# A two-layer gated cross-attention and feed-forward block on one core: a key projection, an addition, a scaling and the terms of a value tile change places

## The reference

```python
x = x + tanh(g_xattn[0]) * _L0_xattn_ref(layernorm(x), ctx, ...)  # fake_quant(x1) @ fake_quant(ctx), 8 bits
x = x + tanh(g_ffn[0])   * _L0_ffn_ref(layernorm(x), W_int, scale_i32, bias)   # per-token 8 bit, dequantized W, + bias
x = x + tanh(g_xattn[1]) * _L1_xattn_ref(layernorm(x), ctx, ctx, Wq, Wk, Wv, Wo)  # 32 heads of 32, 8 KV heads
x = x + tanh(g_ffn[1])   * _L1_ffn_ref(layernorm(x), weight_packed, scales)    # 4 bit weights

def fake_quant(x, scale, zp):
    q = jnp.clip(jnp.round(x / scale + zp), 0.0, 255.0)
    return (q - zp) * scale
```

## Time and profile before

| what | value |
|---|---|
| median of 3 runs | 850.35 us (848.24 to 850.78) |
| the profiled execution, its own time | 850.95 us |
| span of its records, first to last instruction | 849.1 us |
| TensorE (matmul) | 822.5 us, 97% of the span |
| VectorE | 590.0 us, 69% |
| GpSimd | 536.4 us, 63% |
| ScalarE | 448.9 us, 53% |
| mean granted clock of TensorE | 0.996 of full speed |

### The profile page before, as it was taken

The page is one execution under the profiler, slowest core; times in us unless marked ns, Lnnn a source line. Parts: engine busy times, 40 slices in busy tenths (PEclk is TensorE's granted clock), DMA queues, the critical chain, the costliest instruction groups (busy, mean ns, idle before and its releaser), DMA issues.

```text
span 849.1 us, 14036 instructions
## 1 busy us (share of the span) xinstructions
PE 822.5 (97%) x4498; PEld 332.2 (39%) x4498; DVE 590.0 (69%) x850; ACT 448.9 (53%) x742; POOL 536.4 (63%) x235
## 2 busy tenths in 40 slices
PE   8999989899999999999999999999999889999998
PEld 7766634344444432222222222222222213444443
DVE  5897768988378678888888888888888400555522
ACT  4445466565422257767777777777777771111200
POOL 5556158956243437988888988888988885222300
PEclk9999999999999999999999999999999999999999
DMA  7999953428995116445456444546544434122331
GB/s 251 230 288 293 278 123 108 105 57 151 251 231 152 64 59 135 109 103 107 105 113 134 109 108 100 121 96 133 127 96 94 100 63 87 25 50 49 62 137 74
DMA packets 120823, 107.81 MB, mean 127 GB/s; under 512 B 85325, under 2 KB 105805, under 8 KB 116685
## 3 DMA queue, kind: packets, MB, share of 16 engines
q1 hardware_dynamic: 115120, 71.59, 32.7%
q0 software_dynamic: 4608, 33.56, 19.5%
q10 hardware_dynamic: 1052, 2.10, 0.9%
HBM read 41.55 MB, written 12.58 MB: 64 GB/s over the span
## 4 chain that ended last, share of the span: by engine, by line
PE 65%; DMA 10%; POOL 8%; DVE 5%; issue 4%; DVEq 3%; ACT 3%; SPq 1%; ACTq 0%; POOLq 0%
PE sbank L1673 9%; PE sbank L1684 9%; PE mpair L1613 9%; POOL wraw L604 7%; DMA tail<-wraw 5%; PE sbank L1483 3%; PE sbank L1485 3%; PE sbank L1484 3%; PE sbank L1751 3%; PE sbank L1768 3%; PE sbank L1753 3%; PE sbank L1766 3%; PE sbank L1755 3%; DVEq L958 3%; DMA regD<-wraw 3%
## 5 line engine op out<-in xcount | busy, mean ns | idle before, releaser
L1345 DVE TENSOR_REDUCE mx<-mpair 128x1 f32<-128x1024 f32 x256 | 302.3, 1217 | 60.8 <-PE mpair L1613 59.8
L900 ACT ACTIVATE regC<-sbank 128x512 f32<-128x512 f32 x512 | 277.9, 595 | 105.8 <-PE sbank L1673 102.6
L1673 PE MATMUL sbank<-regD 98*128 98x512 f16 x512 | 178.2, 384 | 6.6 <-ACT regC L900 5.6
L604 POOL TENSOR_TENSOR wraw<-regC 128x2048 f32<-128x2048 f32 x32 | 148.5, 4641 | 31.4 <-DMA tail<-wraw 24.7
L1613 PE MATMUL mpair<-regD 96*128 96x512 f16 x512 | 155.9, 380 | 1.0 <-DVE mx L1345 0.4
L1684 PE MATMUL sbank<-regC,regD 128*32 128x512 f32 x1024 | 136.4, 605 | 1.0 <-ACT regC L900 1.0
L1673 PEld LDWEIGHTS sbank<-regD 98*128 98x128 f16 x512 | 48.5, 97 | 184.8 <-ACT regC L900 147.3
L604 POOL TENSOR_TENSOR regD<-regC 128x2048 f32<-128x2048 f32 x16 | 76.5, 4781 | 13.6 <-ACT regC L900 13.5
L604 POOL TENSOR_TENSOR tail<-regC 128x2048 f32<-128x2048 f32 x16 | 77.0, 4814 | 0.0
L1613 PEld LDWEIGHTS mpair<-regD 96*128 96x128 f16 x512 | 47.6, 98 | 54.4 <-DVE mx L1345 13.9
L497 POOL TENSOR_SCALAR xT_lo<-xT_lo,sc 128x1024 f32<-128x1024 f32 x16 | 31.1, 1944 | 36.4 <-DVE X L1010 28.2
(11 more groups left out here) (186 smaller groups left out, 1282.1 us busy)
## 6 DMA issues: line engine op xcount, KB each, us to landing
regD<-wraw POOLq DMA_DIRECT2D x16, 1024.0 KB, 7.0
tail<-wraw POOLq DMA_DIRECT2D x16, 1024.0 KB, 7.0
xT_lo<-in_ctx SPq DMA_DIRECT2D x16, 512.0 KB, 5.1
wraw<-in_L_ffn_W_int SPq DMA_DIRECT2D x8, 512.0 KB, 4.3
X<-in_x SPq DMA_DIRECT2D x4, 1024.0 KB, 7.0
wraw<-in_L_xattn_Wq SPq DMA_DIRECT2D x8, 512.0 KB, 3.7
wraw<-in_L_xattn_Wo SPq DMA_DIRECT2D x8, 512.0 KB, 4.3
regD<-q_hi_scratch SPq DMA_DIRECT2D x32, 128.0 KB, 2.4
```

The lines of the kernel that those rows point to most:

```text
L604: nc.gpsimd.tensor_tensor(p_sum[pr if pr < 3 else 1][:, :, :], probs[:, (2 * pr) % 4, :, :], probs[:, (2 * pr) % 4 + 1, :, :], ALU.add).th ...
L900: nc.scalar.activation(probs[:, kt % 4, h, :], bank[4 + h % 2], ACT.Exp, scale=SCALE).then_inc(s["exp_ok"], 1)
L1345: v.tensor_reduce(mx[m][:, bass.ds(n, 1)] if par is not None else mx[m][:, n:n + 1], slot[:, :, :], AX.XY, ALU.max).then_inc(s["mx_red"], 1)
L1673: pe.matmul(bank[4 + h % 2], kst[par][0:98, kt * P:(kt + 1) * P], qst[par][0:98, h * 512:(h + 1) * 512], start=True, stop=True).then_inc(s ...
```

## The change

Six edits, none of which changes what is computed.

1. TensorE: `k_proj(3, 1)` and the weight transposition 7 come ahead of the four column sums instead of behind them. ScalarE and VectorE follow: `k_out(3, 1)` and `k_low(3, 1)` come right behind those of key tile 0, the copies of the sums are split in two pairs and put between the steps of the last two tiles' norm, the weight tile 7's parts move back (`wd_low`) and its scaling forward (`wd_scale`).
2. GpSimd: the context passes of tiles 11 and 15 also wait for the affine values of the pair of x tiles that is in work; `add_c2(1)`, and with it all adds after tile 0, waits for the last of the eight roundings.
3. The scaling of the bias moves from VectorE (after a2's statistics) to ScalarE (after the rounding of tile 1). On ScalarE `wq_high(0)` moves ahead of the first deviation, `wq_high(1)` behind it, and none is left after the first rounding.
4. VectorE, chunks 1 and 2: `ctx_low(u + 3)` moves ahead of the second `stats` and `ln1_affine`.
5. `newton`: the reciprocal is also written to a PSUM column (`rr_p`), and the small products that read two SBUF operands read this one instead.
6. TensorE: the first value tile does, for each half of the depth, the products with the high half of the weights first, and waits for the low half only then.

```diff
@@ GpSimd: ctx_affine, add_c2
+                if u > 2 * TB and u % TB == TB - 1:
+                    pool.wait_ge(s["ln1_aff"], u // TB - 1)
                 nc.gpsimd.tensor_scalar(cx[:, u % TB, :], cx[:, u % TB, :], IS2, Z2, ALU.mult, ALU.add)
...
                 pool.wait_ge(s["ln1_u"], t + 1)
+                if t == 1:
+                    pool.wait_ge(s["ln1_q"], T)
                 nc.gpsimd.tensor_tensor(X[:, t, :], X[:, t, :], c2[:, t // TB, :], ALU.add).then_inc(s["x_c2"], 1)
@@ ScalarE: last chunk
             k_out(c, 0, False)
             ln1_out(T - 3)
-            for n in range(2 * B):
-                c2_out(n)
-            wd_high(T - 1)
+            k_out(c, 1, False)
             ln1_affine(T - 2)
+            c2_out(0)
+            c2_out(1)
             ln1_out(T - 2)
             ln1_affine(T - 1)
-            k_out(c, 1, False)
+            wd_high(T - 1)
             ln1_out(T - 1)
+            c2_out(2)
+            c2_out(3)
@@ ScalarE: stages A and B
+            def bias_scale():
+                act.wait_ge(s["bias_in"], 16)
+                nc.scalar.activation(biasB, biasB, ACT.Copy, scale=TF0).then_inc(s["bias_ok"], 1)
+
+            wq_high(0)
             ln2_deviation(0)
-            wq_high(0)
+            wq_high(1)
             for t in range(T):
                 ln2_round(t)
+                if t == 1:
+                    bias_scale()
...
-                if t < 5:
+                if 1 <= t < 5:
                     wq_high(t + 1)
@@ VectorE: chunk
                 wd_low(2 * c + 1)
+                ctx_low(u + 3)
                 stats(2 * c - 1, 2 * c - 1).then_inc(s["ln1_stat"], 1)
                 d()
                 ln1_affine(c - 1)
-                ctx_low(u + 3)
                 ctx_round(u + 2)
@@ VectorE: last chunk
             wd_low(T - 2)
+            wd_scale(T - 1)
             ln1_stats(c - 1)
             ln1_affine(c - 1)
-            wd_scale(T - 1)
             ln1_round(T - 4)
             ln1_stats(c)
             ln1_round(T - 3)
             ln1_affine(c)
             k_low(c, 0)
-            wd_low(T - 1)
+            k_low(c, 1)
             ln1_round(T - 2)
             ln1_round(T - 1)
-            k_low(c, 1)
-            def bias_scale():
-                dve.wait_ge(s["bias_in"], 16)
-                v.tensor_scalar(biasB, biasB, TF0, None, ALU.mult).then_inc(s["bias_ok"], 1)
-                d()
+            wd_low(T - 1)
@@ VectorE: newton, ln3_affine
                 v.reciprocal(rr[:, c], sd[:, c])
-                d()
-                v.tensor_tensor(ra_p[:, c], rr[:, c], rr[:, c], ALU.mult)
+                v.reciprocal(rr_p[:, c], sd[:, c])
+                d()
+                v.tensor_tensor(ra_p[:, c], rr_p[:, c], rr[:, c], ALU.mult)
...
-                v.scalar_tensor_tensor(out=mr_p[:, c], in0=mv[:, c, 0], scalar=0.5, in1=rr[:, c], op0=ALU.mult,
+                v.scalar_tensor_tensor(out=mr_p[:, c], in0=mv[:, c, 0], scalar=0.5, in1=rr_p[:, c], op0=ALU.mult,
@@ TensorE: first value tile, called instead of v_proj(0, 0)
+            def first_v_proj():
+                pe.wait_ge(s["ct_lo"], 2)
+                for half in range(2):
+                    if half == 1:
+                        ctx_turn(1, 2)
+                    ks = range(4 * half, 4 * half + 4)
+                    pe.wait_ge(s["wkv_hi"], half + 1)
+                    for k in ks:
+                        pe.matmul(bank[0][:, 0:KV], ctxT_hi[:, k, 0:P], wv_hi[:, k, :], start=(k == 0), stop=False)
+                        pe.matmul(bank[0][:, 0:KV], ctxT_lo[:, k, 0:P], wv_hi[:, k, :], start=False, stop=False)
+                    pe.wait_ge(s["wkv_lo"], half + 1)
+                    for k in ks:
+                        m = pe.matmul(bank[0][:, 0:KV], ctxT_hi[:, k, 0:P], wv_lo[:, k, :], start=False,
+                                      stop=(k == KD - 1))
+                m.then_inc(s["kv_mm"], 1)
@@ TensorE: chunks 1 to 3
                 k_proj(c, 0)
-                if last:
-                    for n in range(2 * B):
-                        c2_sum(n)
-                wd_turn(2 * c + 1)
+                if not last:
+                    wd_turn(2 * c + 1)
                 k_proj(c, 1)
+            wd_turn(KD - 1)
+            for n in range(2 * B):
+                c2_sum(n)
```

More of the change, by code:

```diff
@@ L169, in build @@
                   + [("b", t) for t in range(3, T)])
-        ra_p, am_p, step_p, mr_p, rh_p = (bank[7][:, T * i:T * i + T] for i in range(5))
+        ra_p, am_p, step_p, mr_p, rh_p, rr_p = (bank[7][:, T * i:T * i + T] for i in range(6))
         acc_sb = y[:, 0:512]
@@ L1287, in _ @@
                 a_stats(t)
-                if t == 2:
-                    bias_scale()
             ln2_scales(0)
@@ L1495, in v_proj @@
                     pe.wait_ge(ctl[n % 2], 16 * (n // 2 + 1))
-                if u == 0:
-                    pe.wait_ge(s["wkv_lo"], 1)
                 if c > 0:
@@ L1501, in v_proj @@
                     pe.wait_ge(s["ct_lo"], 2 * j)
-                def between(i):
-                    if u == 0 and i == 2:
-                        ctx_turn(1, 2)
-                        pe.wait_ge(s["wkv_lo"], 2)
                 t0 = (c % 2) * 512
@@ L1509, in v_proj @@
                       lambda k: ctxT_lo[:, k, bass.ds(t0 + j * P, P)], lambda k: wv_hi[:, k, :],
-                      lambda k: wv_lo[:, k, :], between).then_inc(s["kv_mm"], 1)
+                      lambda k: wv_lo[:, k, :]).then_inc(s["kv_mm"], 1)
+            def first_v_proj():
[13 more added lines that the diff above has]
+                m.then_inc(s["kv_mm"], 1)
             def k_proj(c, m):
@@ L1544, in _ @@
             idle_products(12)
-            v_proj(0, 0)
+            first_v_proj()
             ctx_turn(2, 4)
```

## The result

| | before | after |
|---|---|---|
| median, us (executions) | 850.94 (8) | 843.44 (8) |
| lowest to highest, us | 847.9 to 853.8 | 841.13 to 847.49 |
| profiled execution: its own time, us | 850.95 | 841.13 |
| ratio after to before | | 0.9912, 95% interval 0.9893 to 0.9931 |

The change wins 7.5 us in the medians; forecast were 7.1 and 843.3 us. The profiled execution of after is the fastest of its eight, so the two profiles stand 9.8 us apart, more than the change is worth. To read them, I cut each at two starts of TensorE: that of the first product of stage A, and that of the first product of the query projection (its line is L1483 before and L1490 after).

What follows compares the result with a forecast made beforehand. TensorE, 97% busy, could win only idle and half-clock time, chiefly a 3.9 us key-tile wait, then VectorE's in-order chain. -3.9 - 1.7 - 2.1 + 1.0 - 0.4 = -7.1 us gave 843.3 us; eight times in ten 841.1 to 847.0.

Steps and rivals of the forecast that it cites:

- My own sign of being wrong: Wait over 2 us at first B or fourth A product behind it, front losing over 2, or query projection not moving.
- The wait of the second product, -3.9: Stage A: with the last key projection ahead of the sums, TensorE's 3.9 us wait for the key tile goes.
- The held adds: GpSimd, stage A: adds held behind the eighth rounding cause no wait; that rounding takes 0.69 us rather than 2.44.
- The clock, -1.7: Behind the second A product's wait: clock stays up, its 16 matmuls fall to 3.5 us; bounds 0 and -1.9.
- VectorE's chain, -2.1: Stage A to B: of 3.6 us of later TensorE waits, 1.5 stay lost to clip collisions; bounds -3.6 and +4.
- The small multiply: VectorE's chain to stage B: 2.08 us becomes 0.16 with one PSUM operand, plus a 0.17 reciprocal; 1.8 us saved.
- the bias scale: Moved to ScalarE: VectorE then waits about 1.3 us for ScalarE, so only some 0.2 of 1.5 us are won.
- Context subtraction, +1.0: Front, chunks 1 and 2: moved forward it delays the affine chain and weight scale; 1.0 us lost, bounds 0 and +2.0.
- First value tile, -0.4: Front: high-half products fill TensorE's 1.0 us wait for the low half; part is eaten later; bounds 0 and -2.7.
- B: Stages A and B: clip collisions on VectorE's chain take back half, gain 4.3 us, 846.0 us; chance 0.17.
- C: Nothing measurable, under 2.55 us, about 849.5: query projection waits for low transfers behind the last clip, or order fails; chance 0.09.
- D: Slower: GpSimd becomes the bound with 50 us of work from 116.7 on; 853.4 us at 13 us late; chance 0.03.

Runs made afterwards that it cites:

- the second pair: Second profiles: the changed kernel run again unchanged (median 844.61 us) beside the kernel before run once more (852.02 us, one execution).
- e1: Kernel before with only the new order of the last key projection, on all engines: 848.9 us against 852.1, ratio 0.9956.
- e2: Changed kernel with the order of the last key projection put back, other five edits kept: 846.07 us, ratio to before 0.9927.
- e7: Changed kernel without the hold of GpSimd's adds behind the last rounding: 847.7 us against 851.06 for the kernel before, ratio 0.9948.
- e12: Changed kernel run again unchanged, on a third chip: 844.61 us, ratio to before 0.9916.
- e4: Changed kernel with the first value tile in its old order: 844.53 us, ratio to before 0.9915.
- e9: Changed kernel with the context subtraction back behind the affine step and the weight scale ahead of VectorE's rounding: 843.78 us, ratio to before 0.9913.
- e8: Changed kernel with the small multiplies as before, both operands in SBUF and no second reciprocal: 850.11 us, ratio to before 0.9982.

## Why the prediction was right, step by step

**The time and the sum.** 843.3 was forecast, 843.44 and 844.61 came. The sum for stages A and B was 7.7 us (3.9 + 1.7 + 2.1); the profiles give 9.7 and 7.5, 8.6 on the mean. The front was to lose 0.6 (1.0 less 0.4); it lost 1.3 and 2.9, 2.1 on the mean. So 0.9 us too little was forecast as won in the stages and 1.5 too little as lost in the front, and the two nearly cancel. That the median came to within 0.2 us of the forecast is luck in this, and in two more things: the kernel before came out at 850.94 and not at the 850.35 that I subtracted from, and the rest behind stage B, which I had at nothing, is 1.5 and 1.6 us shorter in the two pairs. My own sign of being wrong, a front that loses more than 2 us, is met in the second pair (2.9) and on the mean.

**The wait of the second product, -3.9.** Right in size (between the starts of the two products 7.51 us became 3.46), and e1 shows that the new order is enough. It is not needed for most of it: in e2 the short roundings take 2.9 us of the wait away without it. The late key tile has two causes in a row, its place in the order and the long roundings ahead of it. The held adds cost nothing, as I said; a gain of their own I did not count, and e7 shows one, ahead of the first B product.

**The clock, -1.7.** Seen in the first pair (from the second product to the fifth's start 12.07 us became 10.36). In the second profile of before the same interval is 10.37 behind a 3.3 us wait. It is a loss in some executions and not a fixed price; I should have kept the bound 0 as a case and not only as a bound. On the chip of e12 the mean granted clock over all executions is 0.9966 for the kernel before (11 executions) and 0.9970 for the changed one (6): over the whole kernel the clock gave back little.

**VectorE's chain, -2.1, mis-sized.** It gave 3.9 and 3.6: 2.3 and 2.0 us between the sixth and the seventh A product, and 1.6 in both pairs behind the last one. The clips lost about what I had placed (1.00, 1.07, 1.66 and 1.24 us, 3.3 over four times 0.43; 3.0 by my list; four clips lie ahead of the first B output, and not five), but the first one did not hold up the first B product, and only 0.5 us of the 3.6 of waits was left, where I had left 1.5: the first B output came 34.3 us behind the first A product (33.2 by my count without collisions) and its bank was wanted at 34.7 (34.5 by my count). The small multiply was counted as 1.8 us of VectorE. Its undoing costs 4.8: 2.3 of wait, 1.7 of clock behind it, 0.8 later. That is the largest single edit. Of the bias scale, VectorE waits 0.7 us for ScalarE (1.3 said); what its move wins (0.2 said) is not shown.

**Context subtraction, +1.0, the step that failed.** I took it as a delay by its own length and set its bounds at 0 and 2.0. The loss of its cover under ScalarE's affine step is as I said (0.77 us). The wait came out at 2.7 and 3.4 us where I wrote "about 1 us of wait". Part of it is not lost: TensorE came there 1.4 and 2.0 us sooner, and the transposes start 1.3 us later than before in the first pair and 0.1 in the second. What I had no term for is what follows such a wait: in the second pair the front loses 2.8 of its 2.9 us to the clock behind it. Also missed were the wait that the subtraction itself has for its buffer, 0.2 us in both profiles of the changed kernel and 1.8 to 1.9 in three others, and the 0.8 us that the weight scale takes longer beside GpSimd in the first pair (in the second it takes 1.97 us before and 2.04 after).

**First value tile, -0.4.** TensorE is 2.4 us earlier at its fifth group of transposes (19.35 against 21.74), but e4, with the old order and the clock at 1.00, is there at 19.85 and e1, with the same two, at 21.20; the ten profiles with the new order lie between 18.8 and 20.7. How much of the 2.4 is the order's and how much the clock's of the earlier trace rows stays open. TensorE then waits for the weight scale, and e4 shows no difference at the end. No gain of this edit is shown.

**The rivals.** B (the collisions take half) was near in the clips and wrong in their effect. C's sequence, the low transfers behind the last clip, did not hold the gain back: the query projection starts 8.4 us sooner, 1.3 less than stage A and B won because of the front. Of D nothing was seen.

## What to carry over

An instruction on an in-order engine may be moved forward only past the point where its own inputs and its own buffer are ready; look up what it would wait for at its new place, not only what it delays. When two edits aim at one wait, each may cover most of it alone: undo each by itself before pricing it. Price a wait of TensorE with the clock behind it, as a chance. And cut profiles at landmarks: the middle stretch repeated to 0.02 us in two profiles of the changed kernel, while the whole time went over 6 us. Take its noise from versions that don't touch the stretch (here up to 1.3 us), and not from that one pair.

## What the runs showed that I had not expected

Whether the granted clock falls behind a wait of TensorE differs between executions. At the weight transposes it stayed at 1.00 behind waits of 1.3, 1.6, 1.7, 2.0, 2.7 and 3.0 us, fell behind 2.3 (e9), 2.7 (e7) and 3.4, 5.3, 5.5 and 6.2; behind the wait of the second A product it fell after 3.9 and stayed after 3.3; behind that of the seventh it stayed after 2.8 in the kernel before and fell after 2.8 in e8. The Trainium skill (TensorE: Matmul & The Clock Gate, "What's actually happening") says that the number of slow matmuls at a kernel's start changes from run to run; here the clock behind a wait in the middle does so. And six small multiplies, of 0.17 us each where nothing is beside them, were worth more (5.6 to 6.0 us in the medians) than the order of a projection of 24 matmuls (3.2 us in e1).
